# Order of the feed-forward tiles in a decoder layer: ten shared tiles in one block ahead of the 79 expert tiles, in place of four, eight expert tiles and six alternating pairs

## The chip, the core and the metric

The kernel runs on one core of a Trainium2 chip. The metric is the device time of one execution in microseconds. Three executions of the kernel before gave 907.54, 907.58 and 910.18 us; the median is 907.58 us.

## What is computed

The layer has 2048 tokens of 256 numbers. Two attention parts come first (a linear one, then cross-attention to 1601 context rows), each with a residual and a layer norm. Behind them stands the feed-forward part, the only one that the change touches:

```python
probs = softmax(xf @ gate_w.T)                  # 16 experts
top_w, top_idx = top_k(probs, 4); top_w /= sum(top_w)
h1, h3 = xf @ w1[e].T, xf @ w3[e].T             # hidden size 128
moe_out = sum over the 4 chosen e of top_w * ((silu(h1) * h3) @ w2[e].T)
shared  = (silu(xf @ sw1.T) * (xf @ sw3.T)) @ sw2.T
x = layernorm(x + moe_out + shared)
```

## The kernel before

The program of each engine is written out by hand; engines meet at semaphores only. PE is TensorE, DVE is VectorE, ACT is ScalarE, POOL is GpSimd, and SP issues most DMAs. Every engine works through its own program strictly in order, POOL's and SP's DMAs included.

**The expert stage.** Each of the 2048 tokens goes to 4 experts, so there are 8192 rows. They are written to the DRAM buffer `sorted_d` at places given by `slots`, so that each of 79 tiles of 128 rows belongs to one expert. These scatters are indirect DMAs on POOL (`scatter`, L853), one for each block of 128 tokens and each of the 4 choices. The first 12 of the 16 blocks of tokens are scattered while attention is still running. The last 4 blocks can't be: their gate values come out of the last chunk of attention. Their 16 scatters (`SCATTER_AT`, stage 2 in the code) stand inside the expert stage, and so does DVE's chain that computes their slots (gate centre, softmax, top, ranks, slots; DVE's last step is L2143, which releases the first scatter).

**The list of work.** The stage works through a list `WORK` of 95 tiles: 16 "shared" tiles (128 tokens each, with the weights of the shared expert) and 79 "expert" tiles v0 to v78. A loop counter i runs on every engine from -3 to 98. In iteration i, PE turns the rows of entry i+3 (L1690), does the first product of entry i+1 (`inner`, L1728), turns the activation of entry i-1 (L1736) and does the second product of entry i-3 (`outer`, L1746). ACT copies and computes silu; for an expert tile it writes the weighted result to `y_out` (L1239, `take_out`), for a shared tile DVE adds it to `sums` (L2294, `add_shared`).

POOL's part of iteration i is, in this order: a scatter of the last blocks when i is 14 to 29, and `give(i - 4)`. For an expert tile, `give` is one indirect DMA (L928) that writes the 128 finished rows of `y_out` to `given_d`; for a shared tile it is nothing. What stands at fixed i (scatters, the last blocks' gate chain, POOL's write of the second order list, L919, at i = 42) doesn't depend on what kind of tile is at i.

**The buffers.** Expert tiles are loaded by SP (L711) into `x_in`, which has 18 slots. `give` reads the destinations of its rows from the same slot, so a slot is free only when that DMA has landed:

```python
X_SLOTS, Y_SLOTS, Y_SIGNALS = 18, 12, 6
# SP, load_tile, for expert tile v:
if v == FULL_FIRST:                       # v == 33
    all_sorted(STAGES - 1)                # all 16 last scatters landed
if v >= X_SLOTS:
    sp.wait_ge(y_stored[v % Y_SIGNALS], 16 * ((v - X_SLOTS) // Y_SIGNALS + 1))
...
# POOL, every iteration:
if i in SCATTER_AT:
    sort_row(STAGES - 1, *SCATTER_AT[i])
if 0 <= i - 4 < len(WORK):
    give(i - 4)
```

So the load of v waits for the landing of the give of v-18, and PE's L1690 of v waits for the landing of that load. Tile v33 is entry 43 of the list, in both kernels, and is turned at i = 40. SP issues loads in the order of v.

**Behind the experts.** From i = 66 on DVE adds up the four rows that each token got (`add_given`, L2304 to L2306, loads by SP, L723), and a norm and the store follow.

Of the kernel before, what the change touches and what calls it, by code (L numbers as in the profile page):

```python
# [100 lines left out]
def mixed(pattern, shared, expert):  # L101
    return [("shared", next(shared)) if kind == "s" else ("expert", next(expert)) for kind in pattern]


_shared, _expert = iter(range(TILES)), iter(range(SLOT_TILES))
LATE = 6
LATE_FIRST = TILES - LATE
WORK = mixed("s" * 4 + "e" * 8 + "se" * 6 + "e" * 65 + "s" * LATE, _shared, _expert)
X_SLOTS = 18
X_SIGNALS = 12  # L110
CLEARED = 12
# [28 lines left out]
assert SLOT_TILES <= LISTED <= P and X_SLOTS % Y_SIGNALS == 0 and Y_SLOTS % Y_SIGNALS == 0  # L140
assert len(WORK) == TILES + SLOT_TILES and KNOWN_OWNERS % EXPERT_LOAD == 0
assert LASTK > 0 and REST * TPC <= CHUNK and UNITS == PER_STEP * KT


def decoder_layer(nc, a, out):
    with ExitStack() as ctx:
# [308 lines left out]
        IN_TURN = []  # L455
        for i in range(-AHEAD, len(WORK) + BEHIND):
            IN_TURN.extend(LAST.get(i, ()))
            if i + AHEAD < len(WORK):
                IN_TURN.append(("tile", i + AHEAD))
# [6 lines left out]
        def shared_until(i):  # L466
            return sum(kind == "shared" for kind, _ in WORK[:i])

        def experts_until(i):
            return sum(kind == "expert" for kind, _ in WORK[:i])  # L470

# [3 lines left out]
        for i, t in COMBINE_AT.items():  # L475
# [5 lines left out]
            else:  # L481
                i = len(WORK) - TILES + t
                assert WORK[i] == ("shared", t)
# [2000 lines left out]
```

## Time and profile before

| what | value |
|---|---|
| median of three executions | 907.58 us |
| the profiled execution | 907.53 us |
| its span (first to last instruction) | 905.6 us |
| granted TensorE clock over the span | 0.994 |
| PE busy | 875.7 us, 97% |
| DVE, ACT, POOL busy | 703.0, 668.4, 322.3 us |
| chain that ended last | PE 79%, DVE 12%, ACT 5% |

The profiled execution's time is its span and 1.9 us around it. Engine times are from one execution. The expert stage begins at about 729 us of the span, where PE turns the rows of the first shared tile. All times of the rows below are microseconds from the start of the span.

### The profile page before, as it was taken

What the parts mean: (1) busy time and instruction counts of PE and PEld (TensorE: products, weight loads), DVE (VectorE), ACT (ScalarE), POOL (GpSimd) and SP (SyncE); (2) the same over time, 40 slices, a digit from 0 to 9 for tenths busy, and PEclk for the clock granted to TensorE, in tenths of its full rate; (3) what the DMA queues carried; (4) which work ended last, traced back from release to release, by engine and by line L of the source; (5) the groups of instructions that cost most, each with busy time, mean ns of one, the idle gap of its engine ahead of it and who ended that gap; (6) DMA issues with size and microseconds to landing.
All of it is one profiled execution on the core that took longest, in us unless ns stands there. A gap on an engine that the chain in (4) does not pass through costs nothing.

```text
span 905.6 us, 19295 instructions
## 1 busy us (share of the span) xinstructions
PE 875.7 (97%) x6987; PEld 501.4 (55%) x6987; DVE 703.0 (78%) x1122; ACT 668.4 (74%) x1491; POOL 322.3 (36%) x385
## 2 busy tenths in 40 slices
PE   8999999999999999999999999999999999999995
PEld 5776776544444444444444444444444367888883
DVE  5336789899999998899998898998889446311587
ACT  4435664378888888888888788888888956677773
POOL 1916787630000001020000020005654644777674
PEclk9999999999999999999999999999999999999997
DMA  9307638403335221011011011011334743466795
GB/s 324 100 1 141 135 100 135 114 26 89 102 96 172 78 71 27 9 26 31 9 26 32 8 25 26 14 26 38 108 112 128 196 124 111 141 173 203 259 327 178
DMA packets 69781, 91.56 MB, mean 101 GB/s; under 512 B 15224, under 2 KB 52602, under 8 KB 69656
## 3 DMA queue, kind: packets, MB, share of 16 engines
q1 hardware_dynamic: 62008, 68.52, 27.0%
q0 software_dynamic: 6928, 18.82, 5.7%
q10 hardware_dynamic: 752, 2.98, 2.0%
q8 instruction: 58, 0.95, 0.5%
q14 instruction: 35, 0.29, 0.1%
HBM read 48.80 MB, written 39.40 MB: 97 GB/s over the span
## 4 chain that ended last, share of the span: by engine, by line
PE 79%; DVE 12%; ACT 5%; issue 2%; POOL 1%; DMA 1%; POOLq 0%; DVEq 0%; ACTq 0%
PE psum L1545 21%; PE psum L1454 17%; PE psum L1531 9%; PE psum L1728 9%; DVE mpart L1916 7%; PE psum L1746 4%; ACT region L1273 3%; PE psum L1374 2%; PE psum L1690 2%; PE psum L1339 2%; PE psum L1505 2%; PE psum L1471 2%; PE psum L1568 1%; PE psum L1347 1%; ACT region L1132 1%
## 5 line engine op out<-in xcount | busy, mean ns | idle before, releaser
L1273 ACT ACTIVATE region<-psum 128x512 f32<-128x512 f32 (+1 forms) x832 | 447.8, 610 | 77.1 <-PE psum L1531 63.3
L1916 DVE TENSOR_REDUCE mpart<-psum 128x2 f32<-128x1024 f32 x384 | 462.0, 1222 | 25.9 <-PE psum L1454 21.3
L1545 PE MATMUL psum<-region 128*32 128x256 f32 (+1 forms) x3120 | 248.8, 390 | 1.8
L1454 PE MATMUL psum<-kstack,qstack 63*128 63x512 f32 (+1 forms) x1024 | 211.2, 441 | 4.9 <-DVE mpart L1916 3.7
L1454 PEld LDWEIGHTS psum<-kstack,qstack 63*128 63x128 f32 x1024 | 88.1, 184 | 173.9 <-issue 123.8
L1531 PE MATMUL psum<-qstack,kstack 64*128 64x512 f32 (+1 forms) x832 | 174.1, 406 | 0.7 <-ACT region L1273 0.7
L1545 PEld LDWEIGHTS psum<-region 128*32 128x32 f32 (+1 forms) x3120 | 64.1, 108 | 107.6 <-issue 83.7
L1531 PEld LDWEIGHTS psum<-qstack,kstack 64*128 64x128 f32 (+1 forms) x832 | 111.2, 181 | 16.2 <-ACT region L1273 13.2
L997 POOL TENSOR_TENSOR attnT<-num_c,den_c 128x512 f32<-128x512 f32 x7 | 9.0, 1281 | 244.6 <-DMA den_c<-den_d 244.4
L928 POOL DMA_INDIRECT given_d<-y_out,x_in x79 | 77.3, 978 | 37.8 <-ACT y_out L1239 25.8
L1728 PE MATMUL psum<-w_all,xT_in 128*128 x316 | 81.6, 381 | 0.9 <-ACT xT_in L1217 0.5
L2284 DVE SCALAR_TENSOR_TENSOR act_h<-silu_h,psum 128x128 f32<-128x128 f32 x95 | 27.2, 287 | 68.6 <-ACT silu_h L1221 68.0
L1728 PEld LDWEIGHTS psum<-w_all,xT_in 128*128 128x128 f32 x316 | 53.9, 190 | 5.5 <-issue 1.3
L853 POOL DMA_INDIRECT sorted_d<-x_rows,slots x48 | 47.6, 992 | 25.5 <-PE psum L1531 14.2
L1132 ACT ACTIVATE region<-psum,small 128x64 f32<-128x64 f32 x128 | 27.9, 329 | 26.8 <-DVE small L1927 26.7
L1746 PE MATMUL psum<-w_all,actT 128*128 x158 | 47.2, 380 | 0.0
L1221 ACT ACTIVATE silu_h<-psum 128x128 f32<-128x128 f32 x85 | 23.6, 278 | 29.7 <-PE psum L1728 29.6
L1239 ACT ACTIVATE y_out<-psum,x_in 128x256 f32<-128x256 f32 x79 | 37.4, 474 | 7.6
L1217 ACT ACTIVATE xT_in<-psum 128x256 f32<-128x256 f32 x95 | 35.7, 377 | 6.5 <-PE psum L1690 6.3
L1912 DVE TENSOR_REDUCE mpart<-psum 128x8 f32<-128x528 f32 x32 | 22.7, 708 | 13.0 <-PE psum L1454 11.6
L1002 POOL TENSOR_TENSOR x_rows<-proj,x_rows 128x256 f32<-128x256 f32 x12 | 8.3, 688 | 65.2 <-ACT proj L1169 65.1
L837 POOL TENSOR_TENSOR rstd<-var_eps,half_neg 128x1 f32<-128x1 f32 (+1 forms) x20 | 13.2, 658 | 49.8 <-DVE var_eps L2002 37.0
(304 smaller groups left out, 1039.2 us busy)
## 6 DMA issues: line engine op xcount, KB each, us to landing
x_in<-sorted_d SPq DMA_DIRECT2D x79, 129.0 KB, 2.3
sorted_d<-x_in SPq DMA_DIRECT2D x6, 1548.0 KB, 7.9
given<-given_d SPq DMA_DIRECT2D x16, 512.0 KB, 5.8
qstack<-qparts_d SPq DMA_DIRECT2D x96, 64.0 KB, 2.3
qparts_d<-region SPq DMA_DIRECT2D x8, 512.0 KB, 3.0
kparts_d<-region SPq DMA_DIRECT2D x4, 800.5 KB, 9.3
kstack<-kparts_d SPq DMA_DIRECT2D x6, 400.2 KB, 10.2
kstack<-kparts_d ACTq DMA_DIRECT2D x6, 400.2 KB, 14.0
```

Source lines behind the costliest of these rows:

```text
L853: pool.indirect_dma_start(out=sorted_d[:, :], out_offset=bass.IndirectOffsetOnAxis(ap=slots[:, t, j:j + 1], axis=0), in_=row, in_offset=No ...
L928: pool.indirect_dma_start(out=given_d[:, :], out_offset=bass.IndirectOffsetOnAxis(ap=x_in[:, v % X_SLOTS, DIM:DIM + 1].bitcast(I32), axis= ...
L1132: ins = act.activation(qexp[:, i % 2, head], bank(i % 2)[:, head], ACT.Exp, bias=small[:, 32 * (i % 2) + h:32 * (i % 2) + h + 1])
L1217: act.activation(xT_in[:, i % 3, :], turn_bank("tile", i)[:, 0:DIM], ACT.Copy).then_inc(xT_copied, 1)
L1239: act.activation(y_out[:, v % Y_SLOTS, :], bank(2 + i % 2)[:, 0:DIM], ACT.Copy, scale=x_in[:, v % X_SLOTS, DIM + 1:DIM + 2]).then_inc(y_co ...
L1273: act.activation(prob[0:rows_of, s % 3, j, :], ring(n)[0:rows_of], ACT.Exp).then_inc(ring_read, 1)
L1454: mm = pe.matmul(bank(unit_bank(u) + side)[:, at * w:(at + 1) * w], qstack[rows_of, buffer(G), p, t * P:(t + 1) * P], kstack[rows_of, g * ...
L1531: pe.matmul(ring(n)[0:r], kstack[rows, g * PAIRS + p, kt * P:kt * P + r], qstack[rows, buffer(G), p, :], start=True, stop=True).then_inc(r ...
L1545: mm = pe.matmul(bank(NUM_BANK)[VW * j:VW * (j + 1), q], vals[0:r, g, kt, j, :], prob[0:r, s % 3, j, q], start=(kt == 0 and half == 0), st ...
L1728: mm = pe.matmul(bank(6 + i % 2)[:, 0:2 * HID], xT_in[:, i % 3, k * P:(k + 1) * P], part_of(kind, v, k), start=(k == 0), stop=(k == DK - 1))
L1746: pe.matmul(bank(2 + i % 2)[:, 0:DIM], actT[:, i % ACT_SLOTS, :], part_of(kind, v, DK), start=True, stop=True).then_inc(y_done, 1)
L1916: dve.tensor_reduce(mpart[:, G % 2, qt, :, p, n], both, X, ALU.max).then_inc(max_read, 1)
```

## The change

One line, the pattern of the list, in which s is a shared tile and e an expert tile:

```diff
 LATE = 6
 LATE_FIRST = TILES - LATE
-WORK = mixed("s" * 4 + "e" * 8 + "se" * 6 + "e" * 65 + "s" * LATE, _shared, _expert)
+WORK = mixed("s" * 10 + "e" * 79 + "s" * LATE, _shared, _expert)
 X_SLOTS = 18
 X_SIGNALS = 12
```

Expert tiles v0 to v7 move from entries 4 to 11 to entries 10 to 17, v8 to v12 move by 5 to 1 entries, v13 stays at entry 23, and everything from there on stands where it stood. SP's program is the same in both. Three engines' programs show the move at places that the prediction speaks of.

POOL, from the copies of the last rows (L866, iterations 4 to 7) to the last scatter (iteration 29), in the kernel before. L928 is `give`, L853 a scatter of the last blocks:

```order
L866 COPY last_rows<-x_rows 128x4x256 x4
L928 DMA given_d<-y_out,x_in 10496x256 x6
L853 DMA sorted_d<-last_rows,slots 10112x258
L928 DMA given_d<-y_out,x_in 10496x256
L853 DMA sorted_d<-last_rows,slots 10112x258
L928 DMA given_d<-y_out,x_in 10496x256
L853 DMA sorted_d<-last_rows,slots 10112x258 x2
L928 DMA given_d<-y_out,x_in 10496x256
L853 DMA sorted_d<-last_rows,slots 10112x258 x2
```

The same place in the changed kernel:

```order
L866 COPY last_rows<-x_rows 128x4x256 x4
L853 DMA sorted_d<-last_rows,slots 10112x258
L928 DMA given_d<-y_out,x_in 10496x256
L853 DMA sorted_d<-last_rows,slots 10112x258
L928 DMA given_d<-y_out,x_in 10496x256
L853 DMA sorted_d<-last_rows,slots 10112x258
L928 DMA given_d<-y_out,x_in 10496x256
L853 DMA sorted_d<-last_rows,slots 10112x258
```

Six gives (v0 to v5) that stood ahead of the first scatter now stand behind it, and scatters and gives alternate one by one up to the 16th scatter. In both kernels the give right behind the 16th scatter is that of v15.

DVE, in the gate chain of the last blocks (iterations 9 to 12); L2294 is `add_shared`, L2284 the activation of a tile:

```order
 L2062 TENSOR_TENSOR one_hot<-which,ramp 128x256
 L2284 SCALAR_TENSOR_TENSOR act_h<-silu_h,psum 128x128
+L2294 SCALAR_TENSOR_TENSOR sums<-psum,x_rows 128x256
 L2076 TENSOR_REDUCE gate_work<-one_hot 128x64
 L2077 CAST chosen<-gate_work 128x64
```

```order
 L2180 TENSOR_TENSOR late_to<-rank,start 128x64
 L2181 TENSOR_TENSOR over<-rank,step_from 128x256
 L2184 TENSOR_TENSOR over<-over,step_up 128x256
 L2284 SCALAR_TENSOR_TENSOR act_h<-silu_h,psum 128x128
+L2294 SCALAR_TENSOR_TENSOR sums<-psum,x_rows 128x256
 L2193 TENSOR_REDUCE ups<-over 128x64
```

Six additions of shared tiles that stood behind the slots of the last blocks (L2143) now stand ahead of them, one in each iteration from 7 to 12.

PE, at the fifth entry of the list (iterations 1 to 3), before; the TENSOR_LOAD fetches the owners of four expert tiles into registers, which the w_all products need and the w_shared products don't:

```order
L1690 MATMUL psum<-ident,x_in 128x128 x2
L1728 MATMUL psum<-w_shared,xT_in 128x256 x2
L1736 MATMUL psum<-ident,act_h 128x128
L1690 MATMUL psum<-ident,x_in 128x128 x2
L1700 TENSOR_LOAD order_row
L1728 ISA
L1728 MATMUL psum<-w_all,xT_in 128x256
```

In the changed kernel the first three such TENSOR_LOADs stand at iterations 9, 13 and 17 instead of 3, 7 and 12.

## Rows read from the trace of the kernel before

**Rows 1.** Page, part 1: busy time of each engine.
```profile
PE 875.7 (97%) x6987; PEld 501.4 (55%) x6987; DVE 703.0 (78%) x1122; ACT 668.4 (74%) x1491; POOL 322.3 (36%) x385
```

**Rows 2.** Windows: length; busy (count) of PE, PEld, DVE, ACT, POOL; clock, DMA share, GB/s.
```profile
740.00:750.00 10.00, 9.25 (x63) 7.17 (x63) 6.77 (x24) 4.68 (x15) 5.20 (x5) 1.00 0.49 135
...
760.00:800.00 40.00, 40.00 (x224) 33.82 (x223) 15.52 (x58) 27.23 (x93) 29.03 (x31) 1.00 0.45 142
800.00:840.00 40.00, 40.00 (x223) 33.80 (x222) 6.91 (x24) 29.21 (x100) 28.61 (x31) 1.00 0.66 193
840.00:880.00 40.00, 40.00 (x223) 33.84 (x222) 28.72 (x88) 29.46 (x100) 28.67 (x29) 1.00 0.88 304
```

**Rows 3.** Timeline of PE, turns of entries 42, 43 (v33) and 44: start, duration.
```profile
802.70 0.38 PE L1690 MATMUL psum<-ident,x_in 128*128 128x128 f32 x2
...
804.33 0.38 PE L1690 MATMUL psum<-ident,x_in 128*128 128x128 f32 x2
...
805.95 0.38 PE L1690 MATMUL psum<-ident,x_in 128*128 128x128 f32 x2
```

**Rows 4.** Timeline of POOL: first scatter, gives v6, v10, v13, 16th scatter, give v15.
```profile
764.04 0.96 POOL L853 DMA_INDIRECT sorted_d<-last_rows,slots  x1 [1.49 <-DVE slots L2143]
765.31 0.98 POOL L928 DMA_INDIRECT given_d<-y_out,x_in  x1 [0.30 <-issue]
...
779.24 0.96 POOL L928 DMA_INDIRECT given_d<-y_out,x_in  x1 [0.30 <-issue]
...
790.63 0.96 POOL L928 DMA_INDIRECT given_d<-y_out,x_in  x1 [0.30 <-ACT y_out L1239]
...
794.44 0.96 POOL L853 DMA_INDIRECT sorted_d<-last_rows,slots  x1 [0.30 <-issue]
795.70 0.96 POOL L928 DMA_INDIRECT given_d<-y_out,x_in  x1 [0.30 <-issue]
```

**Rows 5.** Timelines of SP, three windows: loads of v28, of v31 and v32, of v33.
```profile
781.79 0.34 SPq L711 DMA_DIRECT2D x_in<-sorted_d  x1
...
794.46 1.83 SPq L711 DMA_DIRECT2D x_in<-sorted_d  x2
...
798.98 2.35 SPq L711 DMA_DIRECT2D x_in<-sorted_d  x3
```

**Rows 6.** Line L711 alone, all 79 loads, issue to landing.
```profile
DMA to landing us min/median/max: 2.0/2.3/6.4
```

**Rows 7.** Timeline of DVE: an addition and what follows, two idle times, the slots.
```profile
741.80 0.42 DVE L2294 SCALAR_TENSOR_TENSOR sums<-psum,x_rows 128x256 f32<-128x256 f32 x1
742.13 1.38 DVE L1998 TENSOR_SCALAR x_rows<-x_rows,meanvar,rstd 128x256 f32<-128x256 f32 x4
...
755.01 0.29 DVE L2284 SCALAR_TENSOR_TENSOR act_h<-silu_h,psum 128x128 f32<-128x128 f32 x1 [0.37 <-ACT silu_h L1221]
...
757.55 0.23 DVE L2161 TENSOR_TENSOR needed<-rank,less_missing 128x64 f32<-128x64 f32 x1 [0.69 <-ACT rank L1212]
...
763.07 0.17 DVE L2143 CAST slots<-which 128x16 int32<-128x16 f32 x1
```

**Rows 8.** Timeline of PE: the product behind the second TENSOR_LOAD, and the ranks.
```profile
749.26 1.13 PE L1728 MATMUL psum<-w_all,xT_in 128*128 x4 [0.50 <-ACT xT_in L1217]
...
756.17 0.27 PE L1616 MATMUL psum<-chosen,before 128*128 128x64 f32 x1 [0.37 <-DVE chosen L2077]
```

**Rows 9.** Timelines: POOL's give of v28, SP's load of v46, PE's turn of v46.
```profile
813.42 0.96 POOL L928 DMA_INDIRECT given_d<-y_out,x_in  x1 [0.30 <-ACT y_out L1239]
...
819.60 0.33 SPq L711 DMA_DIRECT2D x_in<-sorted_d  x1
...
825.48 0.38 PE L1690 MATMUL psum<-ident,x_in 128*128 128x128 f32 x2
```

**Rows 10.** Timelines of the end: POOL's last give, SP's last load of given rows.
```profile
889.90 0.96 POOL L928 DMA_INDIRECT given_d<-y_out,x_in  x1 [0.41 <-ACT y_out L1239]
...
895.08 0.32 SPq L723 DMA_DIRECT2D given<-given_d  x1
```

## The prediction

> **What bounds the kernel now.** I read the page's busy times first: PE is busy 97% of the span, every other engine well below [rows 1]. A share over the span doesn't say what bounds the stage that is changed, so I read the windows of that stage. From 760 to 880 us PE is busy without a gap, at a granted clock of 1.00 [rows 2]. In the timeline of PE one entry takes (805.95 - 802.70) / 2 = 1.625 us, whatever its kind [rows 3]; over longer stretches the same rows repeat every 1.63 us. So from 760 us on the order of the tiles can win nothing: the sum of PE's work is the same. It can only lose, if something that PE needs comes too late. Ahead of 760 us PE has small gaps (9.25 of 10 us busy from 740 to 750 [rows 2]), and there something could be won.
>
> The next view is the one that matters: who is nearly too late? POOL. From its first scatter at 764.04 to the give of v15 at 795.70 it never rests: 25 indirect DMAs later at 31.66 us, so 1.266 us each (0.96 busy, 0.30 of issue between them) [rows 4]. PE takes 1.63 us for an entry, so one DMA for an entry leaves POOL time, and two (2.53 us) don't. And the landing of a give frees the slot into which SP loads the tile that comes 18 expert tiles later. SP issued the load of v33 at 798.98 [rows 5]; with the median landing of 2.3 us [rows 6] it was there at 801.28, and PE turned v33 at 804.33 [rows 3]. The slack is 3.05 us. That is the number on which the change hangs.
>
> **The change on POOL.** Before, six gives (v0 to v5) stood ahead of the first scatter, and behind it, up to the give of v15, 15 further scatters and ten gives (v6 to v15): the 25 steps. In the changed kernel no give stands ahead, since v0 is entry 10 and its give is at i = 14, right behind the first scatter. From the first scatter to the give of v15 there are now 15 further scatters and 16 gives, 31 steps. What the gives wait for is there: `y_out` of an expert tile is written one iteration ahead of its give's place, and POOL falls behind from the start. So the give of v15 comes 6 x 1.266 = 7.6 us later after the first scatter. The time that POOL had for these six gives, ahead of 764 us, is now spent idle.
>
> **The change on DVE.** The first scatter waits for the slots, DVE's step at 763.07. Six additions move ahead of them. An addition shifts what follows it by 0.33 us (741.80 to 742.13) [rows 7]. The first four fall where DVE waits anyway: 0.37 us ahead of the activation at 755.01, and 0.69 us for the ranks at 757.55 [rows 7], and PE itself waited 0.37 us for DVE's choice ahead of the ranks [rows 8]. The last two, in iterations 11 and 12, stand in a gapless run of DVE up to the slots: 2 x 0.33 = 0.66 us. Bounds: 0 if all six hide, 6 x 0.33 = 2.0 if none does. I take 0.66.
>
> **The change on PE and ACT.** Shared tiles need no owners in registers. Behind the second TENSOR_LOAD PE stood 0.50 us [rows 8]; the profile names a copy by ACT as its end, but that product needs an older copy, so I read it as the register load, which PE's queue couldn't run ahead of behind the sixteen small gate products. At most some 0.7 us is saved there with its slower products (1.13 us for four against 1.03 in full flow). But the next thing is the wait of PE for the choice of experts, at 756.17 [rows 8], which hangs on DVE's chain behind the gate products, and those stand ahead of the saved stretch. So PE arrives earlier and waits longer. The later loads of owners fall into full flow, where none costs anything (there is one for every four expert tiles, and PE has no gap from 760 to 880 [rows 2]). I cost it at 0. ACT loses six copies to `y_out` there and gets them back later, between 760 and 800, where it is busy 27 of 40 us [rows 2]: 0.
>
> **The sum.** The first scatter comes 0.66 us later, the give of v15 at 795.70 + 7.6 + 0.66 = 803.96. From that give to SP's load of v33 it took 798.98 - 795.70 = 3.28 us before [rows 4, 5]. For other tiles it was 2.55 (v10 to v28, 779.24 to 781.79) and 3.83 (v13 to v31, 790.63 to 794.46); I take that of the same tile. The load is issued at 807.24 and lands 2.3 us later at 809.54. PE would have turned v33 at 804.33. So PE is **5.2 us** late: 7.6 + 0.66 - 3.05. The tiles ahead of v33 share this delay, since in the alternating part each give comes 2.53 us behind the last one: v29 to v33 each come some 0.9 us later than PE wants. Behind v15 there is one DMA for a tile again, at 1.266 against 1.63 us, and each tile wins 0.36 us of slack back; PE isn't held again, but what it lost stays lost, since it had no gap in which to catch up. The 16 scatters land before the give of v15 does, so v33's second wait (`all_sorted`) adds nothing.
>
> What is late next? The write of the second order list stands in POOL's queue just ahead of the give of v28, and the load of v46 behind it came 6.2 us after that give (813.42 to 819.60), though it was needed only at 825.48 [rows 9]. POOL's backlog carries over: the load comes at 819.60 + 8.26 = 827.86, lands at 830.16, and PE, 5.2 us late, wants it at 830.68. It just fits, by 0.5 us. The end of the kernel hangs on the last expert tile (last give at 889.90, and the last load of given rows 5.18 us behind it at 895.08 [rows 10]); all of that moves with PE. POOL's backlog is gone before: 31 steps take 39.2 us where 16 entries take 26.1, a lag of 13 us, and it shrinks by 0.36 us a tile, so within 37 of the 63 tiles behind v15. So the whole 5.2 us reach the end: 907.53 + 5.2 = **912.7 us**. The profiled execution stands 0.05 us from the median of the runs, so no correction is due.
>
> On the landing of an indirect DMA, this case's rows show 2.55 to 3.83 us from a give to the load that it frees [rows 4, 5]. The Trainium skill, page "DMA: Bandwidth & Descriptors", section "Anatomy of one DMA — SWDGE (gpsimd) path", gives about 2.0 us and the bytes at 436 GB/s, an estimate of 2.3 us for the 128 KB of a give. With it the delay would be about 4.2 us instead of 5.2. The rows decide, and they say that this tile's took longer.
>
> **The rivals.**
> *Not slower: POOL keeps within the slack.* Place: POOL's 31 steps. If the 0.30 us between two DMAs is not work but a wait that a fuller queue hides, a step costs 0.96 us, the 31 steps take 29.8 us, less than the 31.66 of before, and PE is never late: 907.5 us. It decides at (31.66 + 3.05 - 0.66) / 31 = 1.10 us for a step. Against it: the 0.30 stands between all back-to-back DMAs of rows 4. Chance 0.09. Faster would need the front's saving to get past the wait for the choice as well: 906.8 us, still within the bound below; chance of more than 0.3% 0.03.
> *A small stall.* The landings are at their quick end and DVE hides all additions: 7.6 + 0 - 3.05 - 0.73 = 3.8 us, or even less if loads land in the 2.0 us of rows 6; 911 us down to 910. It is the lower end of the forecast.
> *A second stall.* At v46 to v50, behind the order's write, the slack is 0.5 us, and loads that are issued close together may land slower than 2.3 (up to 6.4 [rows 6]). Price 0.5 to 2 us more: 914 us. Chance 0.13.
> *The clock.* PE does 1.63 us of work in 2.53 for some five tiles. If the granted clock fell from 2.4 to 1.2 GHz there, a tile would take 3.26 us, 0.73 more than POOL's pace, for five tiles 3.7 us: 916.4 us. The stage shows 1.00 throughout, also from 740 to 750 with PE at 9.25 of 10 us [rows 2], but no row has PE as idle as here. Chance 0.05.
> The Trainium skill, page "TensorE: Matmul & The Clock Gate", Part 1, says that the clock follows how busy PE has been, and that an idle PE goes to the lower level; by that rule this last case is possible, and no row here shows it.
>
> **How the numbers follow.** The forecast has 0.70: its own range is from 3.8 us (above) to 7.6 + 2.0 - 3.05 + 0.55 = 7.1 us, so 911.3 to 914.6. A measurement of this kernel tells about 0.3% (2.7 us) from no change, so slower begins at 910.3. Slower: 0.70 + 0.13 + 0.05 less 0.04 for small stalls under the bound = 0.84. Same: 0.09 + 0.04 = 0.13. Faster 0.03. The range leaves out not slower and faster (0.12) and the clock's case (0.05): 909.8 to 915.3.
>
> **What the profile would show.** POOL alternates L853 and L928 without rest from about 764.7, 1.27 us a step; the give of v15 at about 804; PE's L1690 waits for DMA in the five or so turns up to v33, about 0.9 us each, with v33 turned near 809.5; from there full flow at 1.63 us and an end 5 us later. It would be wrong if POOL's steps were shorter in alternation, if the first scatter came more than 1 us off, or if a second run of waits stood behind 825 us.

## The result and the profile after

The changed kernel takes **913.75 us** (median of four executions, 913.22 to 915.13), the kernel before beside it 908.37 us (median of four): ratio 1.0061, 95% interval 1.0048 to 1.0073. The forecast was 912.7 us, between 909.8 and 915.3.

The page of the changed kernel, part 1 (busy time of each engine) and the start of part 4 (the chain that ended last), against [rows 1]:

```profile
PE 879.0 (96%) x6987; PEld 501.6 (55%) x6987; DVE 702.4 (77%) x1122; ACT 669.6 (73%) x1491; POOL 322.4 (35%) x385
...
PE 77%; DVE 13%; ACT 4%; issue 3%; DMA 2%; POOL 1%; POOLq 0%; SPq 0%; DVEq 0%; ACTq 0%
```

No engine has more instructions (PE 6987 in both). PE is busy 2.2 us longer ahead of the stage, in the short stretch at the lower clock told of below, and 1.7 us longer in the stage (158.08 us against 156.42), where products behind a gap take 1.11 or 1.13 us in place of 1.03. The rest is in gaps of PE, and the windows say in which stretch (columns as in [rows 2]):

```profile
750.00:760.00 10.00, 9.35 (x65) 7.70 (x58) 8.40 (x42) 5.73 (x18) 0.00 (x0) 1.00 0.11 28
760.00:780.00 20.00, 19.73 (x109) 16.50 (x108) 7.71 (x26) 13.54 (x47) 10.69 (x11) 1.00 0.28 87
780.00:800.00 20.00, 18.68 (x102) 15.30 (x102) 6.89 (x31) 13.97 (x47) 15.19 (x16) 1.00 0.53 161
800.00:840.00 40.00, 37.30 (x201) 30.48 (x202) 6.33 (x22) 26.33 (x88) 30.25 (x33) 1.00 0.63 185
840.00:880.00 40.00, 40.00 (x222) 33.79 (x222) 23.78 (x73) 29.28 (x99) 28.48 (x30) 1.00 0.84 287
```

POOL has no work from 750 to 760 us; PE then misses 4.3 us between 760 and 840 us, where [rows 2] show none, and nothing behind 840. These windows add up the gaps inside PE's records only; the slower products behind them come on top, so turns measure the loss better. They must be counted from the stage's own start, because this execution enters the stage 2.04 us late. PE's first turn of the stage and its turn of the last list entry, timelines of PE, first before, then after:

```profile
729.30 0.65 PE L1690 MATMUL psum<-ident,x_rows 128*128 128x128 f32 x4
...
887.33 0.38 PE L1690 MATMUL psum<-ident,x_rows 128*128 128x128 f32 x2
```

```profile
731.34 0.65 PE L1690 MATMUL psum<-ident,x_rows 128*128 128x128 f32 x4
...
894.93 0.38 PE L1690 MATMUL psum<-ident,x_rows 128*128 128x128 f32 x2
```

The stage takes 163.59 us instead of 158.03: **5.56 us more**. (The 2.04 us are a short stretch at the lower clock: the window 169 to 173 us has a granted clock of 0.57 in this execution. The traces of b_owners, b_pool4 and b_pool6 below show it at the same place, and their stages start at 731.0 to 731.4 us too; it lies ahead of all that the change touches. It makes this execution the longest of the four.)

POOL, from the first scatter to the give of v15, against [rows 4]:

```profile
766.19 1.07 POOL L853 DMA_INDIRECT sorted_d<-last_rows,slots  x1 [16.24 <-DVE slots L2143]
767.57 0.96 POOL L928 DMA_INDIRECT given_d<-y_out,x_in  x1 [0.30 <-issue]
768.84 0.96 POOL L853 DMA_INDIRECT sorted_d<-last_rows,slots  x1 [0.30 <-issue]
...
804.28 0.96 POOL L853 DMA_INDIRECT sorted_d<-last_rows,slots  x1 [0.30 <-issue]
805.55 0.96 POOL L928 DMA_INDIRECT given_d<-y_out,x_in  x1 [0.30 <-issue]
```

POOL waited 16.24 us for the slots and then didn't rest: 805.55 - 766.19 = 39.36 us for 31 steps, 1.27 us each. SP's loads behind that give (seven in one row, the first is v33's), and PE's turns and long waits there:

```profile
808.47 7.71 SPq L711 DMA_DIRECT2D x_in<-sorted_d  x7
```

```profile
799.90 0.41 PE L1690 MATMUL psum<-ident,x_in 128*128 128x128 f32 x2 [1.10 <-DMA x_in<-sorted_d]
...
804.84 1.13 PE L1728 MATMUL psum<-w_all,xT_in 128*128 x4 [0.91 <-ACT xT_in L1217]
...
810.73 0.41 PE L1690 MATMUL psum<-ident,x_in 128*128 128x128 f32 x2 [0.88 <-DMA x_in<-sorted_d]
...
812.47 0.38 PE L1690 MATMUL psum<-ident,x_in 128*128 128x128 f32 x2
813.68 1.13 PE L1728 MATMUL psum<-w_all,xT_in 128*128 x4 [0.83 <-ACT xT_in L1217]
...
815.18 0.38 PE L1690 MATMUL psum<-ident,x_in 128*128 128x128 f32 x2
816.81 0.38 PE L1690 MATMUL psum<-ident,x_in 128*128 128x128 f32 x2
```

The turn of v33 is that at 810.73: 79.39 us into the stage, against 75.03 before [rows 3]: **4.4 us late**. Most of the delay came in three jumps, 1.27, 1.20 and 1.13 us at the turns of entries 38, 41 and 43, not in five even waits of 0.9 us. Two turns on, at 815.18, PE is 5.6 us late, and from there the distance is constant. Between the two stands the second wait, 0.83 us ahead of a product. It is not a DMA's, and the prediction didn't have it. The instruction that stands there is the TENSOR_LOAD of the owners of v32 to v35, and the trace has a record of it on PE's sequencer (PEldq: duration in ns, start in us). Line L1700, first before, then after:

```profile
L1700 PEldq TENSOR_LOAD <-order_row x1: 1062/1062/1062, 803.8 to 803.8; - x1
```

```profile
L1700 PEldq TENSOR_LOAD <-order_row x1: 1208/1208/1208, 812.2 to 812.2; - x1
```

It takes 1.1 to 1.2 us in both. Before, the sequencer began it 2.2 us ahead of PE's turn of entry 44 (805.95), and it was over before PE came to the product behind it. In the changed kernel it began 0.3 us ahead of the same turn (812.47) and ended at 813.4, just ahead of the product at 813.68.

### The profile page after: what moved, and what is told of

Same layout as the page of the kernel before. It is cut to its first block, busy times and chain, and to the rows that moved or that the text cites. A ratio compares the mean times of both kernels' runs of the same rounds, so it can differ in the third digit from the quotient of the medians.

```text
span 913.2 us, 19294 instructions
## 1 busy us (share of the span) xinstructions
PE 879.0 (96%) x6987; PEld 501.6 (55%) x6987; DVE 702.4 (77%) x1122; ACT 669.6 (73%) x1491; POOL 322.4 (35%) x385
## 4 chain that ended last, share of the span: by engine, by line
PE 77%; DVE 13%; ACT 4%; issue 3%; DMA 2%; POOL 1%; POOLq 0%; SPq 0%; DVEq 0%; ACTq 0%
PE psum L1545 20%; PE psum L1454 17%; PE psum L1531 9%; PE psum L1728 8%; DVE mpart L1916 7%; PE psum L1746 4%; PE psum L1374 2%; PE psum L1339 2%; PE psum L1690 2%; PE psum L1505 2%; ACT region L1273 2%; PE psum L1471 2%; PE psum L1568 1%; PE psum L1347 1%; ACT region L1132 1%
## 5 line engine op out<-in xcount | busy, mean ns | idle before, releaser
L928 POOL DMA_INDIRECT given_d<-y_out,x_in x79 | 77.1, 976 | 28.7 <-ACT y_out L1239 14.1
L2284 DVE SCALAR_TENSOR_TENSOR act_h<-silu_h,psum 128x128 f32<-128x128 f32 x95 | 27.1, 287 | 76.4 <-ACT silu_h L1221 73.2
L853 POOL DMA_INDIRECT sorted_d<-x_rows,slots x48 | 47.6, 993 | 25.7 <-PE psum L1531 14.1
L1690 PE MATMUL psum<-ident,x_in 128*128 128x128 f32 x158 | 30.4, 274 | 2.1 <-DMA x_in<-sorted_d 2.0
```

The lines of the kernel that those rows point to most:

```text
L853: pool.indirect_dma_start(out=sorted_d[:, :], out_offset=bass.IndirectOffsetOnAxis(ap=slots[:, t, j:j + 1], axis=0), in_=row, in_offset=No ...
L928: pool.indirect_dma_start(out=given_d[:, :], out_offset=bass.IndirectOffsetOnAxis(ap=x_in[:, v % X_SLOTS, DIM:DIM + 1].bitcast(I32), axis= ...
L1690: mm = pe.transpose(turn_bank("tile", i)[:, k * P:(k + 1) * P], rows[:, k * P:(k + 1) * P], ident[:, :])
```

## The experiments

Five questions: is POOL's queue alone enough to make the loss; does the loss follow the number of steps to the give of v15; what is the wait behind v33; where did the gain at the front go; can the loss be taken back? In the table all times count from PE's first turn of the stage in the same execution, as above. "Steps" are POOL's DMAs behind its first scatter up to the give of v15, with the copies added there; the last four columns are differences from the kernel before (give of v15 at 66.40 there). Entry 45 is two turns behind v33, entry 94 the last.

| kernel | steps | give of v15 | turn of v33 | entry 45 | entry 94 |
|---|---|---|---|---|---|
| b_owners | 25 | -0.74 | -0.73 | -0.73 | -0.73 |
| b_owners3 | 25 | -0.41 | -0.42 | -0.42 | -0.42 |
| b_pool2 | 25 + 2 copies | +2.56 | 0.00 | +0.21 | +0.81 |
| p6 | 27 | +2.29 | -0.38 | +0.06 | +0.21 |
| p6_owners3 | 27 | +1.98 | -0.67 | -0.67 | +0.52 |
| p6_owners3_again | 27 | +2.00 | -0.64 | -0.64 | -0.64 |
| b_pool4 | 25 + 4 copies | +5.02 | +1.85 | +3.05 | +4.29 |
| p8 | 29 | +5.52 | +2.41 | +3.94 | +3.94 |
| changed kernel | 31 | +7.81 | +4.37 | +5.57 | +5.57 |
| a_owners | 31 | +7.82 | +4.79 | +5.34 | +5.63 |
| a_owners3 | 31 | +7.86 | +4.41 | +4.52 | +5.62 |
| b_pool6 | 25 + 5 copies, one ahead | +7.80 | +4.70 | +5.41 | +5.75 |

**b_pool6: the kernel before, with POOL alone delayed.** Six copies between two buffers that no one uses any more, one ahead of each of the first six scatters; list and all other engines as before:

```diff
+                if 14 <= i < 20:
+                    if i == 14:
+                        pool.wait_ge(half_attn_ready, 1)
+                    link(pool.tensor_copy(num_c[:, :, :], den_c[:, :, :]))
                 if i in SCATTER_AT:
```

> The kernel before, with six extra copies of 1024 numbers on POOL (about 1.0 to 1.2 us each, estimated from the copies of the last rows, 1.04 us), one ahead of each of the first six scatters of the last blocks; the list of tiles, and so PE, ACT, DVE and SP, as before. Theory (POOL's queue behind the first scatter is the whole loss): the give of v15 comes some 7 us later, v33 is turned 7 - 3.05 = about 4 us late, and the end moves by 4 to 5 us (ratio 1.0045 to 1.0055). Rival (the loss comes from the new order of tiles on PE, DVE or ACT, with POOL late but covered): within 0.5 us of the kernel before.

913.85 us, ratio 1.0059 [1.0045, 1.0072]: the changed kernel's time without its list, and a little over what was expected. The give of v15 comes 7.80 us later, and v33 and entry 45 are late by what they are late in the changed kernel, to within 0.35 us. So a late POOL is enough, with the list of before. The test isn't as pure as meant, though. DVE's and POOL's timelines around the first copy (lines of this kernel are four higher than before's):

```profile
763.23 0.59 DVE L2197 TENSOR_REDUCE ups<-over 128x64 f32<-128x256 f32 x1
763.85 1.80 DVE L2198 SCALAR_TENSOR_TENSOR late_to<-ups,late_to 128x64 f32<-128x64 f32 x1
765.68 0.42 DVE L2200 TENSOR_TENSOR one_hot<-one_hot,late_to 128x256 f32<-128x256 f32 x1
```

```profile
764.51 1.05 POOL L1063 COPY num_c<-den_c 128x1024 f32<-128x1024 f32 x1
767.61 0.98 POOL L853 DMA_INDIRECT sorted_d<-last_rows,slots  x1 [2.04 <-DVE slots L2147]
```

DVE's small step took 1.80 us while the copy ran; in the changed kernel the same step takes 0.22 us (timeline of DVE, 764.01). It makes the first scatter 1.6 us late, so only some 6.2 of the 7.8 us are the copies' in the queue, and PE itself is 1.34 us late from the turn of entry 19 on. The kernels with two and four copies below are free of this: their copies stand behind the first scatter.

**p8: eight shared tiles ahead.**

```diff
-WORK = mixed("s" * 4 + "e" * 8 + "se" * 6 + "e" * 65 + "s" * LATE, _shared, _expert)
+WORK = mixed("s" * 8 + "e" * 14 + "s" * 2 + "e" * 65 + "s" * LATE, _shared, _expert)
```

> The kernel before with the pattern s8 e14 s2 e65 s6: two gives (v0, v1) ahead of the first scatter, between the six of before and the none of the changed kernel; POOL's chain to the give of v15 has 29 steps in place of 25 (before) and 31 (changed). Theory: 4 x 1.266 = 5.1 us later, less the slack of 3.05: v33 late by about 2 us, plus up to 1.2 us where a load of owners is laid bare behind the wait; less 0.6 us won at the front: +1.4 to +2.6 us against before. Rival (a loss by kind of order, not by count of steps): as the changed kernel, +5.4 us, or as before.

911.73 us, ratio 1.0046 [1.0032, 1.0059]; the stage is 3.94 us longer, more than the 1.4 to 2.6 expected, in the direction of the count. v33 is 2.41 us late, near the 2 us expected. Two terms were missed: the front won nothing (the first scatter came 0.49 us later, where 0.6 us had been counted as won), and the register load behind v33 cost 1.53 us where up to 1.2 had been allowed.

**a_owners and b_owners: the owners fetched one step earlier.** In the changed kernel and in that of before, the TENSOR_LOAD (`load_owners`) moves from just ahead of the product that needs it to the top of the same iteration:

```diff
-                    if v % EXPERT_LOAD == 0:
-                        load_owners(v)
...
+                if 0 <= i + 1 < len(WORK) and WORK[i + 1][0] == "expert" and WORK[i + 1][1] % EXPERT_LOAD == 0:
+                    load_owners(WORK[i + 1][1])
```

> The changed kernel with PE's load of four owners moved from inside the first product of its tile to the top of the same iteration, ahead of the waits for the turned tile. In the changed kernel's trace PE was held not only by the DMAs up to v33 (4.4 us against before at v33's turn, counted from the start of the stage) but 1.2 us more up to v35, where a load of owners stands between the turn and the product. Theory (after each wait the load of owners, hidden in full flow, is laid bare, about 1 us each time): the end moves from +5.5 to about +4.3 us, PE's gaps named by the copy of xT_in (0.91 and 0.83 us) go. Rival (the gaps are part of the wait for the gives and just move): +5.5 us as it was.

> The same edit in the kernel before. There one load of owners stood bare behind the small gate products (0.50 us) and one behind the fourth tile. Theory (DVE's gate chain follows PE there, so what PE wins reaches the slots): the stage is 0.5 to 0.6 us shorter, time -0.5 us, too little for the times but visible in the profile as the turn of entry 14 relative to that of entry 0. Rival, the step of my prediction (PE arrives earlier and waits longer for the choice of experts): the turn of entry 14 stays at 27.8 us behind that of entry 0.

a_owners: 913.46 us, ratio 1.0064 [1.0051, 1.0078]. The gain didn't come: the stage is 5.63 us longer, which is what the rival said, and the theory in this form fell. The wait behind v33 shrank (0.55 us from v33 to entry 45 in place of 1.20), but v33 itself came later.

b_owners: 907.73 us, ratio 0.9997 [0.9988, 1.0007]; a measurement can't tell it from before, but its trace can. Timelines of b_owners: PE's first turn, POOL's first scatter:

```profile
731.39 0.65 PE L1690 MATMUL psum<-ident,x_rows 128*128 128x128 f32 x4
```

```profile
765.41 0.96 POOL L853 DMA_INDIRECT sorted_d<-last_rows,slots  x1 [1.50 <-DVE slots L2143]
```

The scatter comes 34.02 us into the stage; before it was 764.04 - 729.30 = 34.74. PE's turn of entry 14 comes 27.04 us behind that of entry 0, where the rival had it stay at 27.8 (27.76 before). Taking the bare register load out of PE's way at the front brings the slots, the scatter and the whole stage 0.7 us forward.

**a_owners3: the owners fetched three entries ahead, in the changed kernel** (`i + 1` above becomes `i + 3`).

> The changed kernel with the load of four owners three iterations ahead of its first product, ahead of the turn of its own tile. For v32 that puts it ahead of PE's wait for v33, so it runs while PE waits anyway; moved by less than an iteration (the run before this) it stood behind that wait still. Theory: v33 is turned 4.4 to 4.8 us late as before, counted from the start of the stage, and nothing is added up to v35: the stage is 4.4 to 4.8 us longer than before in place of 5.6. Rival (the 1.2 us behind v33 come from the late gives of v16 and v17, not from the load of owners): 5.3 to 5.6 us.

913.03 us, ratio 1.0053 [1.0040, 1.0066]. From v33 (+4.41) to entry 45 (+4.52) 0.11 us is lost in place of 1.20: the wait behind v33 was the register load. But the stage is 5.62 us longer, as before and as the rival's number had it, because the loss comes back further on: 0.34 us at entries 46 and 47, where the early load of the next owners now stands, and 0.76 us at entries 57 to 59. PE's turns of entries 56 to 59 (v46 to v49), timeline of a_owners3:

```profile
830.53 0.38 PE L1690 MATMUL psum<-ident,x_in 128*128 128x128 f32 x2
832.25 0.41 PE L1690 MATMUL psum<-ident,x_in 128*128 128x128 f32 x2
834.45 0.41 PE L1690 MATMUL psum<-ident,x_in 128*128 128x128 f32 x2 [0.30 <-issue]
836.19 0.38 PE L1690 MATMUL psum<-ident,x_in 128*128 128x128 f32 x2
```

From 832.25 to 834.45 an entry took 2.20 us. SP issued the load of v47 at 828.04, behind its own load of the second order list (L678, at 827.13), and it was 4.1 us under way, so it landed only 0.1 us ahead of PE's turn at 832.25. By itself that cost 0.08 us. But PE's sequencer had waited for it, and the next instruction of weight was a register load again, of v48's owners (line L1700 of a_owners3):

```profile
L1700 PEldq TENSOR_LOAD <-order_row x1: 1196/1196/1196, 833.0 to 833.0; - x1
```

It ended at 834.2, and the turn of v48 followed at 834.45. The tile's own load isn't what PE waited for: that of v49, issued behind it, had landed at 833.5. So the place is that of the prediction's second stall, and the price is mostly the register load's.

**b_pool2 and b_pool4: two and four copies** in place of six (iterations 15 and 16, or 15 to 18; the edit is b_pool6's with other numbers).

> The kernel before with two extra copies on POOL, ahead of the second and third scatter of the last blocks. One such copy took 1.27 us of POOL's chain in the run with six, as much as one indirect DMA. Theory (a slack of 3.05 us, then one for one): the give of v15 comes 2.5 us later, within the slack, and the stage is as long as before, within 0.3 us. Rival (every step of POOL costs its share, 5.6 us for six): +1.9 us.

> The same with four copies. Theory: the give of v15 comes 5.1 us later, v33 is turned 2.0 us late, and a load of owners laid bare behind it adds up to 1.4 us: +2.0 to +3.4 us. Rival (a share for every step): +3.8 us.

b_pool2: 908.44 us, ratio 1.0008 [0.9998, 1.0017]; b_pool4: 911.55 us, ratio 1.0034 [1.0021, 1.0047]. The table shows the threshold: 2.56 us of delay vanish at v33, and of 5.02 us 1.85 come through. The first scatter is where it was (34.75 and 34.65 us into the stage, 34.74 before), so here the late v33 comes out of POOL's queue and nothing else. But both stages are longer than expected (0.3 at most for b_pool2, 3.4 for b_pool4), because both lose more behind v33, 0.81 and 2.44 us. Most of it is lost where a register load stands: 0.21 us ahead of entry 45 and 0.55 ahead of entry 61 in b_pool2, 1.20 and 0.42 us ahead of entries 45 and 49 in b_pool4, which loses another 0.82 at a wait of DVE for given rows. By its time alone b_pool4 would fit the rival (a share for every step, +3.8 us) better than the theory; the turn of v33 decides between them, and in b_pool2 it didn't move.

**p6_owners3, p6 and b_owners3: a version that might win.** Six shared tiles ahead, the owners three entries early, then each edit alone.

```diff
-WORK = mixed("s" * 4 + "e" * 8 + "se" * 6 + "e" * 65 + "s" * LATE, _shared, _expert)
+WORK = mixed("s" * 6 + "e" * 14 + "s" * 4 + "e" * 65 + "s" * LATE, _shared, _expert)
```

> The version that the findings point to: pattern s6 e14 s4 e65 s6, so that four gives stand ahead of the first scatter (27 steps of POOL to the give of v15, 2.5 us more than before, within the slack), with the loads of owners three iterations early. Theory: no wait for a DMA in the stage, the front shorter by what PE no longer loses to loads of owners there (0.6 to 0.8 us): ratio 0.999, under what the times can tell, visible in the profile. Rival (the later gives cost again): +0.5 to +1.5 us.

> Six early shared tiles ahead of fourteen expert tiles, then four shared tiles behind them, owners loaded as before: 27 steps on POOL between the first scatter and the give of entry v15. By the queue theory the give comes 2 x 1.27 = 2.5 us later than before, which the wait at entry v33 takes up as it did for two copies (0 to +0.2 us there), and two more additions on VectorE ahead of the slots cost 0 to 0.2 us: 907.5 to 908.6 us. By the theory that each early shared tile ahead of the experts costs in its own right, whatever the queue does, a third of the change's loss comes: +1.9 us, 909.6 us.

> The kernel before with the owners loaded three entries ahead. If the gain of 0.67 us that six tiles with early owners showed from entry 20 on belongs to the owners, it stands here too: 906.9 to 907.5 us. If it belongs to the pattern, this one is at 907.6 to 908.0 us, and the one with six tiles alone is the faster of the two.

p6_owners3: 907.42 us, ratio 0.9995 [0.9986, 1.0003]. p6: 909.02 us, ratio 1.0015 [1.0006, 1.0025]. b_owners3: 907.89 us, ratio 0.9995 [0.9986, 1.0005]. None is measurably faster than before. In the traces v33 is turned 0.38 us earlier by the pattern alone, 0.42 by the early owners alone and 0.67 by both. By its times p6 is 0.95 us slower than before (908.07 beside it), which is above the 907.5 to 908.6 expected and half of the rival's +1.9; its trace is at +0.21 us. Its ten executions reach from 907.71, the profiled one, to 911.05, and the difference stays unexplained. In the trace of p6_owners3 0.67 us were won at v33 and 1.19 lost between entries 80 and 90, where DVE waited for given rows:

```profile
876.54 0.69 DVE L2304 TENSOR_TENSOR given<-given 128x512 f32<-128x512 f32 x1 [2.36 <-DMA given<-given_d]
```

> The same kernel as p6_owners3, for its trace alone. If the 2.36 us for which VectorE waited for given rows near entry 85 came from the schedule, it is there again within half a microsecond, and the stage is 0.5 us longer than before's. If it is a transfer's chance, the wait is absent or at another entry, and the stage is about 0.7 us shorter than before's.

One execution, 907.16 us. The same wait in the same kernel's second trace:

```profile
874.95 0.69 DVE L2304 TENSOR_TENSOR given<-given 128x512 f32<-128x512 f32 x1 [0.68 <-DMA given<-given_d]
```

It is 0.68 us, and PE lost nothing: a stage of 157.39 us, 0.64 less than before. So the late loss was that transfer's chance, and one trace can't tell a schedule by it. It is a place to know, though: the traces of p6, a_owners and b_pool4 lose 0.15, 0.29 and 0.82 us at the same entry 89, with DVE waiting for given rows just ahead of it.

## Why the prediction was right

**POOL's queue.** Right, and the size too: six more steps were put at 7.6 us and took 39.36 - 31.66 = 7.7. The rival in which a step takes 0.96 us in alternation fell: the 0.30 us stood between them again.

**The first scatter.** Right only in the sum of its errors; this is one of the two steps that failed in kind. The prediction put it 0.66 us later, with "PE arrives earlier and waits longer", a front that costs and wins nothing. It came 34.85 us into the stage, 0.1 later. b_owners shows why: what PE saves at the front does reach the slots (0.7 us there). Two additions' 0.66 us less some 0.57 of that saving fits, but that split is worked out, not measured, and p8, where the scatter came 0.49 us later, shows that it doesn't carry over to another list.

**From the give to PE.** Give to load 808.47 - 805.55 = 2.92 us (3.28 assumed), load to turn 810.73 - 808.47 = 2.26 us (2.3 assumed). The landing was thus 0.4 us quicker than in [rows 4, 5]. The Trainium skill, page "DMA: Bandwidth & Descriptors", section "Anatomy of one DMA — SWDGE (gpsimd) path", leads to an estimate of 2.3 us for these 128 KB; the 2.92 us to the load that the landing frees lie between that and the value taken.

**The slack of 3.05 us.** Right. In the six kernels whose v33 came late, the give's delay less v33's is 3.0 to 3.5 us (table: 5.02 - 1.85, 5.52 - 2.41, 7.81 - 4.37, 7.82 - 4.79, 7.86 - 4.41, 7.80 - 4.70). v33 was forecast 5.2 us late and was 4.4: 0.55 us from the first scatter, 0.36 from the landing.

**"PE isn't held again."** Wrong by 1.2 us. The prediction costed all later loads of owners at nothing, since they fall into full flow. Right behind a wait there is no full flow: between v33 and entry 45, where a TENSOR_LOAD stands, 1.20 us were lost in the changed kernel, 1.53 in p8, and 0.11 when it stood three entries earlier. A bare load stood ahead of the product at 804.84 too (0.91 us), hidden among the waits for v31 to v33. That the sum came out so near was luck: 0.9 us too much up to v33 and 1.2 too little behind it, 5.2 forecast, 5.56 measured.

**The second stall.** It didn't add to the changed kernel, in whose trace no turn of v46 to v50 is late again: the load of v46 (issued at 828.90, 2.2 us under way) landed 2.0 us ahead of its turn, where the prediction had 0.5. POOL's backlog was 7.8 us and not 8.26, the load followed its give by 5.6 us and not 6.2, and PE was later. How near the place is, a_owners3 shows.

**The clock.** The rival fell. PE is as idle as here in no row shown of before, 11.02 of 14 us busy, and the granted clock stayed 1.00, the upper of the two levels (windows of the changed kernel):

```profile
798.00:812.00 14.00, 11.02 (x57) 8.13 (x56) 1.73 (x6) 7.50 (x24) 10.65 (x12) 1.00 0.55 169
```

**To the end.** From entry 45 to 94 PE keeps its distance, and the last gives and the end move with it. The whole loss reaches the median, which rose by 5.4 us.

**Still open.** Whether more slots in `x_in` would free the changed list of its loss wasn't tried. Nor was the second stall taken away on its own, and why the times of p6 lie above its trace isn't known.

## What to carry to other kernels

An engine at 35% can set the time: ask how much it must do, in order, between the moment when it may start and the moment at which the bottleneck needs the result, and move nothing from ahead of that stretch into it. Here 3 us of slack took two more DMAs and not four. It didn't take them for nothing: with v33 on time, PE's sequencer had lost part of its lead, and the next register load cost 0.2 to 0.4 us (b_pool2, p6). When one delay is cut, look for the next one close under it before counting on the gain; and where a bottleneck engine falls out of full flow, its register loads, free until then, cost about their full length. Fetching them some entries early helps where they then stand ahead of the wait, and moves the loss where they stand behind another.

## What the runs showed of the hardware

A DVE step on 128x64 values took 1.80 us in b_pool6 while POOL copied 128x1024 values (1.05 us). It took 0.22 in the changed kernel, and 0.22 in b_pool4, where no copy ran beside it. In b_pool6 POOL's copy began 0.66 us behind it (764.51 against 763.85). DVE's record ends at 765.65, POOL's at 765.56. The Trainium skill, page "SBUF — State Buffer", section "Who interferes with whom", says that a VectorE instruction with two SBUF inputs contends with a GpSimd instruction that reads SBUF, over a shared pair of ports that works as an exclusive lock. This step has two such inputs (`ups`, `late_to`), and its end right behind the copy's agrees with that. By the records DVE began first, though, and POOL's starts are rough, so who held the lock isn't shown.

A load of up to four owners on TensorE's sequencer took 0.76 to 1.27 us in the kernel before (20 TENSOR_LOADs of line L1700) and cost nothing that can be seen in full flow (40.00 of 40 us busy [rows 2]), because the sequencer is ahead of PE there: that of v32 began 2.17 us ahead of the turn of entry 44. What it cost elsewhere goes with what was left of this lead, one load in seven traces:

| kernel | began ahead of the turn of entry 44 | took | lost from there to entry 45 |
|---|---|---|---|
| before | 2.17 | 1.06 | 0 |
| p6 | 1.00 | 1.28 | 0.44 |
| b_pool2 | 0.93 | 0.99 | 0.21 |
| b_pool6 | 0.72 | 1.16 | 0.60 |
| changed kernel | 0.27 | 1.21 | 1.09 |
| b_pool4 | 0.22 | 1.16 | 1.09 |
| p8 | 0.00 | 1.24 | 1.42 |

That the sequencer loses its lead by waiting for a DMA's landing is my reading. It fits v47 in a_owners3 (landed at 832.1, the register load began at 833.0 and the turn behind it stood at 834.45), and it fits p6 and b_pool2, where part of the lead was gone though PE's own turn of v33 was on time.
